# Softplus by a shorter chain with its last steps on GpSimd, and D times u written by ScalarE into the banks of y

## What is computed

```
u, z = split(in_proj(x));  u = silu(conv4(u) + conv_b)      # 256 inner channels
dt, B, C = split(x_proj(u));  dt = softplus(dt_proj(dt) + dt_b)
h[n] = exp(dt * A[n]) * h[n] + (dt * u) * B[n]              # 16 states n, scan over time
y = sum_n C[n] * h[n] + u * D
out = out_proj(y * silu(z))
```

## Time and profile before

| | |
|---|---|
| median of three runs | 1202.9 us |
| profiled execution | 1204.23 us, span 1202.5 us, mean granted clock 0.946 |
| TensorE matmul | 1060.3 us, 88% |
| VectorE | 1080.4 us, 90% |
| ScalarE | 874.9 us, 73% |
| GpSimd | 1038.9 us, 86% |
| DMA | 116.79 MB, queues busy 29% |

### The profile page before, as it was taken

How to read it: one execution, slowest core, us unless ns; L and a number is a source line. 1 busy time by engine, 2 the same in 40 slices (tenths; PEclk the granted TensorE clock), 3 DMA queues, 4 the chain that set the end, 5 groups by cost and what they waited for, 6 DMA issues and landing times.

```text
span 1202.5 us, 13235 instructions
## 1 busy us (share of the span) xinstructions
PE 1060.3 (88%) x3786; PEld 639.3 (53%) x3786; DVE 1080.4 (90%) x1220; ACT 874.9 (73%) x1581; POOL 1038.9 (86%) x679
## 2 busy tenths in 40 slices
PE   6889989889889889899898898898898898887987
PEld 4545555555455555555555555555555555444554
DVE  3699999999999999999999999999999999978784
ACT  4678777677777776777787776778868867748653
POOL 3499999899999989989999998989999989858664
PEclk9699989899999899899999898899999998989999
DMA  6232131222322322221322313223222323235451
GB/s 174 81 105 104 64 112 73 94 82 86 112 81 87 112 81 88 86 105 63 112 89 79 111 57 110 81 87 110 83 87 89 103 76 114 94 117 177 146 143 28
DMA packets 64538, 116.79 MB, mean 97 GB/s; under 512 B 34218, under 2 KB 47954, under 8 KB 64466
## 3 DMA queue, kind: packets, MB, share of 16 engines
q1 hardware_dynamic: 64466, 115.96, 29.3%
HBM read 108.47 MB, written 7.47 MB: 96 GB/s over the span
## 4 chain that ended last, share of the span: by engine, by line
PE 39%; ACT 25%; DVE 24%; issue 10%; POOL 1%; DMA 0%; DVEq 0%; POOLq 0%; SPq 0%; ACTq 0%
DVE SCAN L1111 18%; PE Yp L785 17%; PE PP L926 8%; ACT DA L513 7%; DVE SCAN L1076 3%; PE PP L891 3%; PE PP L908 3%; PE PP L866 2%; PE BB L767 2%; ACT GATES L604 2%; ACT GATES L602 2%; ACT GATES L613 2%; ACT GATES L595 2%; ACT GATES L598 1%; ACT GATES L609 1%
## 5 line engine op out<-in xcount | busy, mean ns | idle before, releaser
L448 POOL TENSOR_TENSOR SCAN<-SCAN,CS 128x768 f32<-128x768 f32 x384 | 692.4, 1817 | 70.9 <-DVE SCAN L1111 67.6
L1111 DVE TENSOR_TENSOR_SCAN SCAN<-DA,CAR,SCAN 128x384 f32<-128x384 f32 x672 | 640.8, 1002 | 26.5 <-ACT DA L513 26.4
L785 PE MATMUL Yp<-SCAN,IDENT 128*128 128x384 f32 x1536 | 580.3, 503 | 1.9 <-POOL SCAN L448 1.2
L513 ACT ACTIVATE DA<-UDT,A 128x384 f32<-128x384 f32 x672 | 379.5, 579 | 252.3 <-DVE SCAN L1111 252.2
L785 PEld LDWEIGHTS Yp<-SCAN,IDENT 128*128 128x128 f32 x1536 | 289.3, 196 | 180.1 <-issue 62.6
L1076 DVE TENSOR_TENSOR SCAN<-UDT,BB 128x768 f32<-128x768 f32 x240 | 223.7, 932 | 10.9 <-PE BB L767 10.7
L456 POOL TENSOR_TENSOR SCAN<-UDT,BS 128x768 f32<-128x768 f32 x96 | 174.3, 1815 | 0.0
L926 PE MATMUL PP<-XN,WT 128*128 128x384 f32 x352 | 124.7, 486 | 6.0 <-ACT ZB L626 6.0
L767 PE MATMUL BB<-PT,SEL 96*128 96x384 bf16 x288 | 98.4, 342 | 5.8 <-DVE DA L1076 3.2
L891 PE MATMUL PP<-SQ,MEANW 128*128 128x96 f32 x168 | 37.2, 392 | 72.3 <-ACT SQ L670 72.3
L926 PEld LDWEIGHTS PP<-XN,WT 128*128 128x128 f32 x352 | 66.2, 189 | 54.5 <-issue 8.9
(11 more groups left out here) (212 smaller groups left out, 1256.0 us busy)
## 6 DMA issues: line engine op xcount, KB each, us to landing
CS<-bc_rows SPq DMA_DIRECT2D x96, 768.0 KB, 4.1
BS<-bc_rows SPq DMA_DIRECT2D x24, 768.0 KB, 6.0
out<-XN SPq DMA_DIRECT2D x32, 192.0 KB, 4.3
X<-in_x SPq DMA_DIRECT2D x24, 192.0 KB, 3.5
X<-in_L_ffn_memory_tokens SPq DMA_DIRECT2D x16, 256.0 KB, 3.1
XN<-in_L_ffn_memory_tokens SPq DMA_DIRECT2D x16, 256.0 KB, 3.1
bc_rows<-XDT SPq DMA_DIRECT2D x24, 48.0 KB, 1.5
X<-in_L_ffn_memory_router SPq DMA_DIRECT2D x1, 512.0 KB, 4.5
```

Source lines behind the costliest of these rows:

```text
L448: pool.tensor_tensor(M[:, n1 % MRING], HB[:, n1 % HRING], over_halves(CS[:, n1 % CRING]), ALU.mult).then_inc(m_ready, 1)
L513: act.activation(DA[:, h, 0:T], DT[:, par, h], ACT.Exp, scale=A[:, h, n:n + 1])\
L785: last = pe.matmul(Yp[:, h, 0:T], IDENT[:, :], M[:, n3 % MRING, h], start=n3 == 0, stop=n3 == NS - 1)
L1111: dve.tensor_tensor_scan(HB[:, s % HRING, h], factor, term, CAR[:, ds(J * NS * HALVES + s * HALVES + h, 1)], ALU.mult, ALU.add).then_inc(s ...
```

## The change

Softplus(x) is max(x, 0) + log(1 + exp(-|x|)). The second term was a product of factors from a chain of Ln, Exp and Squares. Now it is a product of E = K exp(-|x|) and Ln(a - s (Ln(1 + cE) + v)^2), with the sign turned: ScalarE does Exp (with ln K as bias), Ln, Square, Ln; GpSimd multiplies in step 10, subtracts in step 11 to make DT, and makes DTU. VectorE's two instructions of step 11 are gone. The buffer SS is gone.

D * u is written by ScalarE into both banks of Yp in its step 2, behind the decays, once VV has been taken; the sum of state 0 waits for it and adds to it. Unit 0 still has the products with diag(D), at the sum of state 0. SQ stands at the beginning of ScalarE's step 10, ahead of the decays, and SQ2 in step 7. The prologue's softplus is shortened alike.

```
-def fit_factors():
-    p = (1.28926229, 1.34076026, -1.527418, -0.43882777, 0.72873143, 0.06986066, 1.76617345)
-    k = p[0] * p[5] * p[6]
-    h1, h2 = 0.5 / p[5], 0.5 / p[6]
-    return p[1], k ** 0.5, h1, k * (h1 * h1 + p[2] / p[5]), p[3], h2, p[4] / p[6] - h2 * h2
-FIT_X, FIT_S, FIT_V, FIT_A, FIT_Z, FIT_W, FIT_B = fit_factors()
-FIT_BIAS = (2.0, FIT_X, -FIT_S * FIT_V, FIT_Z, FIT_W, FIT_A)
+FIT_X, FIT_V, FIT_S, FIT_A, FIT_K = 0.50996051, -3.6873482, -0.046276752, 0.88316448, 0.72962086
+FIT_BIAS = (1.0, FIT_V, FIT_A, math.log(FIT_K))
...
                 if front and s == 10:
-                    pool.wait_ge(fac1_ready, f)
-                    pool.tensor_tensor(SE[:, :, :], SE[:, :, :], SS[:, :, :], ALU.mult).then_inc(m1_done, 1)
+                    pool.wait_ge(log_ready, f + 1)
+                    pool.tensor_tensor(SE[:, :, :], SE[:, :, :], SR[:, :, :], ALU.mult).then_inc(tail_done, 1)
                 if back and s == 11:
                     pool.wait_ge(rstd2_ready, k + 1)
                     pool.tensor_tensor(XC2[:, :, :], XC2[:, :, :], over_q(RSTD2[:, :]), ALU.mult)\
                         .then_inc(xh2_done, 1)
                 if front and s == 11:
+                    pool.wait_ge(tail_done, f + 1)
+                    pool.wait_ge(relu_done, f)
+                    pool.tensor_tensor(DT[:, fp], DT[:, fp], SE[:, :, :], ALU.subtract).then_inc(dt_ready, 1)
                     pool.wait_ge(dt_ready, f + 1)
                     pool.tensor_tensor(DTU[:, fp], DT[:, fp], U[:, fp], ALU.mult).then_inc(dtu_ready, 1)
...
+                if norm and s == 10:
+                    act.wait_ge(xc_ready, g + 1)
+                    positive(act, var_ready, g)
+                    act.activation(SQ[:, :, :], XC[:, :, :], ACT.Square).then_inc(sq_ready, 1)
...
                     act.activation(DT[:, fp], PPT, ACT.Relu).then_inc(relu_done, 1)
-                    act.wait_ge(sp_chain, 3 * f + 1)
-                    act.activation(SE[:, :, :], SE[:, :, :], ACT.Exp, scale=-1.0).then_inc(sp_chain, 1)
                 if front and s == 7:
-                    act.wait_ge(sp_chain, 3 * f + 2)
-                    act.activation(SR[:, :, :], SE[:, :, :], ACT.Ln, bias=FITB[:, 0:1]).then_inc(sp_chain, 1)
-                if front and s == 7:
-                    act.wait_ge(sp_chain, 3 * f + 3)
-                    act.activation(SR[:, :, :], SR[:, :, :], ACT.Exp, scale=-1.0).then_inc(fac_chain, 1)
+                    act.wait_ge(sp_chain, 4 * f + 1)
+                    act.activation(SE[:, :, :], SE[:, :, :], ACT.Exp, bias=FITB[:, 3:4], scale=-1.0).then_inc(sp_chain, 1)
                 if front and s == 8:
-                    act.wait_ge(fac_chain, 3 * f + 1)
-                    act.activation(SS[:, :, :], SR[:, :, :], ACT.Square, bias=FITB[:, 1:2]).then_inc(fac_chain, 1)
-                    act.wait_ge(fac_chain, 3 * f + 2)
-                    act.activation(SS[:, :, :], SS[:, :, :], ACT.Square, bias=FITB[:, 2:3], scale=FIT_S)\
-                        .then_inc(fac1_square, 1)
+                    act.wait_ge(sp_chain, 4 * f + 2)
+                    act.activation(SR[:, :, :], SE[:, :, :], ACT.Ln, bias=FITB[:, 0:1], scale=FIT_X / FIT_K).then_inc(sp_chain, 1)
                 if front and s == 9:
-                    act.wait_ge(fac1_square, f + 1)
-                    act.activation(SS[:, :, :], SS[:, :, :], ACT.Identity, bias=FITB[:, 5:6], scale=-1.0)\
-                        .then_inc(fac1_ready, 1)
+                    act.wait_ge(sp_chain, 4 * f + 3)
+                    act.activation(SR[:, :, :], SR[:, :, :], ACT.Square, bias=FITB[:, 1:2]).then_inc(sp_chain, 1)
                 if front and s == 10:
-                    act.activation(SR[:, :, :], SR[:, :, :], ACT.Square, bias=FITB[:, 3:4]).then_inc(fac_chain, 1)
-                    act.wait_ge(fac_chain, 3 * f + 3)
-                    act.activation(SR[:, :, :], SR[:, :, :], ACT.Square, bias=FITB[:, 4:5]).then_inc(fac2_ready, 1)
+                    act.wait_ge(sp_chain, 4 * f + 4)
+                    act.activation(SR[:, :, :], SR[:, :, :], ACT.Ln, bias=FITB[:, 2:3], scale=FIT_S)\
+                        .then_inc(log_ready, 1)
...
+                if main and s == LAG - 1 and not at(J, 0):
+                    act.wait_ge(v_ready, J)
+                    for h in range(HALVES):
+                        last = act.activation(Yp[:, h, 0:T], U[:, par, h], ACT.Copy, scale=DV[:, h:h + 1])
+                    last.then_inc(du_ready, 1)
+                if back and s == 7:
...
                 act.wait_ge(sp_chain, 2)
-                act.activation(SR[:, :, :], SE[:, :, :], ACT.Ln, bias=FITB[:, 0:1]).then_inc(sp_chain, 1)
+                act.activation(SR[:, :, :], SE[:, :, :], ACT.Ln, bias=FITB[:, 0:1], scale=FIT_X).then_inc(sp_chain, 1)
                 act.wait_ge(set_pe, 4)
                 act.activation(XDT0[DTROW:XROWS, :], ST0[DTROW:XROWS, 8:9], ACT.Copy).then_inc(set_act, 1)
                 act.wait_ge(sp_chain, 3)
-                act.activation(SR[:, :, :], SR[:, :, :], ACT.Exp, scale=-1.0).then_inc(fac_chain, 1)
+                act.activation(SR[:, :, :], SR[:, :, :], ACT.Square, bias=FITB[:, 1:2]).then_inc(sp_chain, 1)
                 act.wait_ge(res2_ready, 1)
                 act.activation(PT[:, 0], XQ[0:DTROW, :], ACT.Copy).then_inc(parts_ready, 1)
-                act.wait_ge(fac_chain, 1)
-                act.activation(SS[:, :, :], SR[:, :, :], ACT.Square, bias=FITB[:, 1:2]).then_inc(fac_chain, 1)
+                act.wait_ge(sp_chain, 4)
+                act.activation(SR[:, :, :], SR[:, :, :], ACT.Ln, bias=FITB[:, 2:3], scale=FIT_S).then_inc(log_ready, 1)
                 act.wait_ge(set_pe, 5)
                 act.activation(TL, ST0[:, 40:42], ACT.Abs).then_inc(set_act, 1)
-                act.wait_ge(fac_chain, 2)
-                act.activation(SS[:, :, :], SS[:, :, :], ACT.Square, bias=FITB[:, 2:3], scale=FIT_S)\
-                    .then_inc(fac1_square, 1)
                 act.wait_ge(set_act, 7)
                 act.activation(TL, TL, ACT.Exp, scale=-1.0).then_inc(set_act, 1)
-                act.wait_ge(fac1_square, 1)
-                act.activation(SR[:, :, :], SR[:, :, :], ACT.Square, bias=FITB[:, 3:4]).then_inc(fac_chain, 1)
                 act.wait_ge(set_act, 8)
                 act.activation(TR, TL, ACT.Ln, bias=LOGB[:, 0:1], scale=1.0 / LOG_C).then_inc(set_act, 1)
-                act.wait_ge(fac_chain, 3)
-                act.activation(SR[:, :, :], SR[:, :, :], ACT.Square, bias=FITB[:, 4:5]).then_inc(fac2_ready, 1)
...
                     pe.wait_ge(m_ready, N - LAG + 1)
-                    if s == LAG:
-                        positive(pe, v_ready, J)
+                    if s == LAG and at(J, 0):
+                        for h in range(HALVES):
+                            pe.matmul(Yp[:, h, 0:T], DD[:, h], U[:, par, h], start=True, stop=False,
+                                      skip_group_check=True)
+                    elif s == LAG:
+                        pe.wait_ge(du_ready, J)
                     for h in range(HALVES):
                         last = pe.matmul(Yp[:, h, 0:T], IDENT[:, :], M[:, n3 % MRING, h],
-                                         start=n3 == 0, stop=n3 == NS - 1)
+                                         start=False, stop=n3 == NS - 1,
+                                         skip_group_check=True)
                     last.then_inc(ysum_done, 1)
-                if main and s == 10:
-                    for h in range(HALVES):
-                        pe.matmul(Yp[:, h, 0:T], DD[:, h], U[:, par, h], start=False, stop=False)
...
-                if front and s == 11:
-                    dve.wait_ge(fac2_ready, f + 1)
-                    dve.wait_ge(m1_done, 2 * f + 1)
-                    dve.scalar_tensor_tensor(out=SE[:, :, :], in0=SR[:, :, :], scalar=FIT_B, in1=SE[:, :, :],
-                                             op0=ALU.add, op1=ALU.mult).then_inc(m1_done, 1)
-                    dve.wait_ge(relu_done, f)
-                    dve.wait_ge(m1_done, 2 * f + 2)
-                    dve.tensor_tensor(DT[:, fp], DT[:, fp], SE[:, :, :], ALU.add).then_inc(dt_ready, 1)
...
-                dve.wait_ge(fac1_square, 1)
-                dve.scalar_tensor_tensor(out=SE[:, :, :], in0=SS[:, :, :], scalar=-FIT_A, in1=SE[:, :, :],
-                                         op0=ALU.add, op1=ALU.mult).then_inc(m1_done, 1)
-                dve.wait_ge(fac2_ready, 1)
-                dve.wait_ge(m1_done, 1)
-                dve.scalar_tensor_tensor(out=SE[:, :, :], in0=SR[:, :, :], scalar=FIT_B, in1=SE[:, :, :],
-                                         op0=ALU.add, op1=ALU.mult).then_inc(m1_done, 1)
-                dve.wait_ge(m1_done, 2)
+                dve.wait_ge(log_ready, 1)
+                dve.scalar_tensor_tensor(out=SE[:, :, :], in0=SR[:, :, :], scalar=FIT_K, in1=SE[:, :, :],
+                                         op0=ALU.mult, op1=ALU.mult).then_inc(tail_done, 1)
```

(16 more changed lines are left out.)

1 line of the change is left out of this document (removed).

## The result

The changed kernel takes 1267.08 us (median of four runs, 1263.7 to 1267.4) against 1202.75 us for the kernel before (median of four): a ratio of 1.0524, interval 1.0499 to 1.0548. The forecast was 1235 us, in a range from 1192 to 1260, so the result lies above the range. The direction and the ring of waits came as written. The clock did not: it costs more than twice what was forecast, and a good part of that at a place that the forecast did not name. The kernel is 64 us slower in place of 32.

The account below looks back on a forecast made before the run. VectorE was taken to bound the kernel, GpSimd close behind. New waits add 15 us over twenty units, the prologue takes off 2.5, clock falls add 21: together +33 us, forecast 1235 us, range 1192 to 1260.

Parts of the forecast that it names:

- the ring of waits: VV to GpSimd's product 24.28 us, product to M 15 19.25, TensorE to VV 1.56: 45.1 us, plus VectorE's delay.
- The clock: TensorE idles 3.39 us before the sum of state 0; its clock then falls in half the units, 2.1 us each: 21 us.
- What goes from VectorE: L1157 and L1161, 2.56 us, and the 1.12 us wait before scan 8 go: 3.68 us per unit.
- The third GpSimd instruction: GpSimd's subtraction adds 1.78 us per unit, while L464 shortens from 1.72 to 0.99 us.
- The wait for the Ln: GpSimd's product waits nearly 3 us for ScalarE's last Ln in step 10; product to M 15 takes 19.25 us.
- D times u: ScalarE's copies behind decay 3 take 1.08 us; state 0's sum starts 3.39 us later, delaying VectorE by 2.3 us.
- The ring without clock falls: The steady unit with TensorE at 2.4 GHz: 45.1 + 2.3 = 47.4 us, against 46.65 before.
- The ends: Outside the twenty steady units: the prologue gains 2.5 us, the last three units change by nothing.
- Rival (c): TensorE's clock falls in every unit after the idle stretch before the sum of state 0: 1257 us, at worst 1275; 6%.
- The 1.00 of the followed unit: Old unit 562.60 to 608.39 us kept full clock despite 3.48 us idle; held against a fall in each unit.
- Rival (d): D times u is hidden by slack, delay below 1.6 us: 1189 us at 1.0 us, 1169 at nothing; 20%.

Follow-up runs that it names:

- the tail alone: The changed kernel with D times u taken back to the two products with diag(D) on TensorE; 1182.58 us, 0.9822 of the kernel before.
- the run with both fillings: The changed kernel with unused identity products filling TensorE's idle stretches before the sums of states 0 and 11; 1218.83 us, 1.013 of the kernel before.

## Why the prediction was right or wrong

- **What goes from VectorE, 3.68 us.** Right to 0.1 us. With the tail alone VectorE works 41.8 us in a unit against 44.23, 2.43 less (worked out as 2.56), and the stall of 1.12 us before scan 8 is gone.
- **The third GpSimd instruction.** Right: L463 takes 1812 ns. And the shorter one came: all of L458, minimum, median and maximum in ns, against the earlier trace rows:

```profile
L458 POOL TENSOR_TENSOR XC<-XC,RSTD x24: 990/1002/1020, 124.1 to 1260.7; 128x384 f32<-128x384 f32 x24
```

  1002 ns where the median was 1714. The rule of the Trainium skill, "SBUF — State Buffer", section "Who interferes with whom", is borne out in both directions: without L1157 and L1161 beside it this GpSimd instruction is never long, and in the run with the subtraction on VectorE it is VectorE's instruction that is (1.44 us).
- **The wait for the Ln.** Right in place and price: the product waits 2.94 us, and from it to M 15 are 19.31 us (618.88 to 636.40 + 1.79), worked out as 19.25.
- **D times u.** Right. The two copies take 1.07 us, worked out as 1.08:

```profile
595.64 1.07 ACT L623 ACTIVATE Yp<-UDT,DV 128x384 f32<-128x384 f32 x2
```

  The sum of state 0 starts 4.55 us after VV (4.50), XC2 12.08 us after VV (12.2), TensorE's idle stretch is 3.30 us (3.39). The delay is 26.52 − 24.36 = 2.2 us, from the run with both fillings and the one without D times u, worked out as 2.3. It does not arise at XC2 alone, as the sum had it: in the unit from 592.30 VectorE waits at scan 4, drive 6 and XC2 in turn, and only the total is the same.
- **The ring without clock falls**, 47.4 us: the run with both fillings has 47.5 in each unit.
- **The clock: here it failed.** The step said that TensorE's clock would fall behind the one idle stretch of 3.39 us, in half of the units, for 2.1 us: 1.05 us per unit, 21 us. The runs showed 2.37 us per unit, at two places: 26 us of the 32 that were missed. The larger part, 20 us, is a stretch that the sum did not have. It listed what is queued behind GpSimd's product and said that TensorE waits for each M, but not that TensorE would so stand idle a second time, 2.39 us before the sum of state 11, with its own fall: 1.23 us in 16 units, 0.99 per unit. The other part, 7 us, is the first stretch, where the measured term is 1.62 us in 17 of 20 units, 1.38 per unit. There the frequency was too low and the price too high, and the one error hid much of the other. I had read 5 in 6 from the units of before, for a stretch of 3.48 us, and took a half with no row that supports it.
- **The ends.** The prologue gave 3.3 us (2.5), the last three units cost 1.2 (0). Not all of the 3.3 need come from ScalarE's shorter chain: the granted clock up to the first VV is 0.93 against 0.89 before. The no-fall unit was 47.55 and not 47.4: 3 us. With the 26 us this is the miss, 30 of 32 us.
- **The rivals.** Rival (c), a fall in every unit at 1257 us, was the nearest and had the least chance of all, 6%. Its number was near in part by luck: it put 2.1 us on every unit at one place, and measured are 1.62 and 1.23 us at two. Its page, "TensorE: Matmul & The Clock Gate" of the Trainium skill, section "HAM oscillation", which tells of a loop whose clock falls in each round, came out nearer than my half: 17 of 20 at the first place. The 1.00 of the followed unit, which I held against it, is one unit in six. Rival (d) was wrong for the change as made, and right for the copies one place earlier. The 20% on it and the half of the units had a common root: I drew back from what the rows gave.
